# Eleven of the Vector engine's additions, between attention and the expert layer, given to GpSimd, with the order of stages kept

## The chip, the cores and the metric

The kernel runs on one core of one Trainium2 chip. The metric is the device time of one execution in microseconds (us), the median of three runs. In the rows and below, PE is TensorE, DVE is VectorE, ACT is ScalarE, POOL is GpSimd and SP is SyncE.

## The reference

The input x is 16 images of 64 channels and 16x16 pixels. A grouped, split-attention convolution block with a residual comes first. Its output is read as tokens: 256 pixels, each with 64 channels, for each of the 16 images. Over the images (axis 0 of `t`) runs a causal attention, then an expert layer with a router:

```python
x = _L0_conv_ref(x, ...)
t = _to_tokens(x)
t = t + _L1_attn_ref(_ln_t(t), L1_attn_fc_w, L1_attn_fc_b, L1_attn_score_w)
t = t + _L1_ffn_ref(_ln_t(t), L1_ffn_Wr, L1_ffn_br, ...)

def _causal_attend(H, e):
    # C[t] = sum over s<=t of softmax(e[s]) * H[s]
    ...
def _L1_ffn_ref(x, Wr, br, W1, ...):
    feat = jnp.mean(x, axis=0)
    w = jax.nn.softmax(feat @ Wr + br, axis=-1)
    h = jnp.einsum('bfd,edh->bfeh', x, W1) + b1
    ...
    return jnp.einsum('bfed,fe->bfd', y, w)
```

Two pieces matter here. The second layer norm works on the tokens with the attention's context added, centred over channels. The router works on the mean of the normalised tokens over the 16 images.

## The kernel before, in words

All arrays fit into the on-chip memory. The images are worked in four quarters, k = 0 to 3, of four images each. A quarter's token tensors are 128 partitions (pixels) by 512 elements (two halves of the pixels, q, by four images, by 64 channels).

One string, `ORDER` (L71 to L87), names every stage as `name.k`. Each engine walks through it and issues only those stages that it has a function for, so the string fixes the order of instructions on every engine. Engines meet only through semaphores. A wait holds everything behind it on the same engine.

The stages that matter for a quarter k:

- `ln1`, `hn`: first layer norm. ACT squares, DVE reduces (L675, L676), POOL raises the variance to the power -1/2 (`power`, L331), and DVE multiplies (L681) the centred tokens `xc` into `hn`.
- `hch`, `fc`, `score`: TensorE and ACT make the attention scores. `coef`, `att` (L690 to L708): DVE makes the coefficients and the first form of the context `ctxs`.
- `scan` (`scan_context`, L720): DVE adds the running context, image by image, in eight small instructions of 128x64. The last raises `ctx_ready`.
- `cen` (`add_to_centred`, L727): `xc` += `ctxs`, 128x512, and raises `centred2`.
- `ln2`: ACT squares the new `xc` (`squares2`, L423), DVE reduces it (L675), POOL takes the power (L331). `xn2`: DVE multiplies (L681) `xc` into the normalised tokens.
- `xt`: TensorE transposes them (L943), ACT copies them into `xs` (L428).
- `xr` (`sum_pairs`, L740 to L745): running sum of `xs` over image pairs, 128x256. Quarter 0 needs one addition and each other quarter two, `xpart` and then `xsum`. The last total feeds `logits` (TensorE L967), from which the routing weights are made.
- `l1.n`, `l2.n` (L1008, L1021): the first and second expert layers, 32 units each. Between them the ReLU is on ACT (L446), and for every second one of the first twenty on DVE (`d1.0` to `d1.9`, L753). ACT does the ReLU behind the second layer (L452).
- `mix` (DVE L783, TensorE L1033) weighs with the routing weights and applies the third layer, and `finish` (L790) adds up the result.

The part of the order around the change reads:

```python
    outp.3 hch.1 fc.1 heat.5 att.0 scan.0 gn4.3 heat.6 cen.0 hn.2 gn4f.3 ln2.0 x1.3 t2.0 hch.2 coef.1 xn2.0 score.1 att.1 tok.3 scan.1
    fc.2 d1.0 xt.0 cen.1 l1.0 l1.1 ln1.3 d1.1 xc.3 score.2 ln2.1 l1.2 l1.3 l2.0 l2.1 coef.2 l1.4 l1.5 hn.3 l2.2 l2.3 d1.2 att.2 xn2.1
    hch.3 l1.6 scan.2 l1.7 fc.3 xt.1 cen.2 d1.3 xr.0 ln2.2 l2.4 l2.5 score.3 l1.8 coef.3 d1.4 l1.9 l2.6 xr.1 l2.7 l1.10 l1.11 l2.8 xn2.2
    l2.9 d1.5 att.3 d1.6 l1.12 scan.3 cen.3 l1.13 l2.10 d1.7 l2.11 xt.2 ln2.3 l1.14 l1.15 l2.12 l2.13 l1.16 d1.8 xn2.3 l1.17 l2.14 l2.15
    l1.18 l1.19 d1.9 xr.2 xt.3 l2.16 xr.3 l2.17 l1.20 l1.21 t2.1 logits.0 l2.18 l2.19 l1.22 l1.23 t2.2 wt.0 l2.20 l2.21 wb.0 wb.1 l1.24
```

Of the kernel before, what the change touches and what calls it, by code (L numbers as in the profile page):

```python
# [22 lines left out]
ALU = mybir.AluOpType  # L23
# [5 lines left out]
P = 128  # L29
# [13 lines left out]
Q = 2  # L43
# [4 lines left out]
BQ = B // NQ  # L48
# [41 lines left out]
def conv_attention_experts(nc: bass.Bass, x: bass.AP, params: bass.AP, row_params: bass.AP, conv1_w: bass.AP, out: bass.AP):  # L90
# [6 lines left out]
    with ExitStack() as ctx:  # L97
        def sb(name, shape, dt=F32):
            return ctx.enter_context(nc.sbuf_tensor(name, shape, dt))

        def sem(name):
            return ctx.enter_context(nc.semaphore(name))
# [26 lines left out]
        xc = sb("xc", [P, NQ, Q, BQ, C])  # L129
        ctxs = sb("ctxs", [P, NQ, Q, BQ, C])  # L130
        xs = sb("xs", [P, NQ, Q, PQ, P])
# [34 lines left out]
        def tile(name, rows, *dims):  # L166
            n = 1
            for d in dims:
                n *= d
            if name not in small_names:  # L170
                small_names[name] = sb("s_" + name, [P, n])
            t = small_names[name][0:rows, 0:n]
            if len(dims) == 2:
                return t.rearrange("p (a b) -> p a b", a=dims[0])
            if len(dims) == 3:
                return t.rearrange("p (a b c) -> p a b c", a=dims[0], b=dims[1])
            return t
# [12 lines left out]
        def sem_list(*names):  # L190
            return [sem(n) for n in names]
# [20 lines left out]
        tok_in_psum, square_ready, hn_ready, ctx_ready = sem_list("tok_in_psum", "square_ready", "hn_ready", "ctx_ready")  # L212
        hch_in_psum, hch_ready, fc_done, qch_ready = sem_list("hch_in_psum", "hch_ready", "fc_done", "qch_ready")
        exps_in, exps_ready = sem_list("exps_in", "exps_ready")
        centred_kept, centred2, square2_ready, xn2_ready = sem_list("centred_kept", "centred2", "square2_ready", "xn2_ready")
        ctx_turned, ctx_added = sem_list("ctx_turned", "ctx_added")
        xt_ready = sem("xt_ready")
        pairs_added, xsum_ready = sem_list("pairs_added", "xsum_ready")
        xs_ready = sem("xs_ready")
# [48 lines left out]
        def rstd(name):  # L268
            n, rows, cols = var_tiles[name]
            return tile(n + "r", rows, cols)  # L270
# [5 lines left out]
        def by_pixel_half(t, k):  # L276

            return t[:, pairs_of(k), :].rearrange("p i (q n) -> p q i n", q=Q)

        def flat(bank_):  # L280

            return bank_[:].rearrange("p (q i n) -> p q i n", q=Q, i=PQ)
# [9 lines left out]
        def merged(t, k):  # L292

            return t[:, k].rearrange("p q b c -> p (q b) c")
# [7 lines left out]
        def context_at(k, q, t):  # L302

            return 2 * (k * BQ + t - 1) + q + 1
# [5 lines left out]
        @block.sync  # L310
        def _(sp):
            for n in range(PAIRS // 2):
                pairs = slice(2 * n, 2 * n + 2)
                sp.dma_start(xin[:, pairs, :], x_pairs[pairs].rearrange("b p n -> p b n")).then_inc(x_loaded[n], 16)
            sp.dma_start(w1[:], conv1_w).then_inc(conv1_w_loaded, 16)
            sp.dma_start(par[:, n_early:], params[:, n_early:]).then_inc(params_loaded, 16)
            for s in range(STRIPS):
                sp.dma_start(row_par[s * STRIP:(s + 1) * STRIP], row_params).then_inc(rows_loaded, 16)

            for k in range(NQ):  # L320
                sp.wait_ge(res_ready, k + 1)
                sp.dma_start(out_pairs[pairs_of(k)].rearrange("b p n -> p b n"), res[:, pairs_of(k), :]).then_inc(out_stored, 16)
            sp.wait_ge(out_stored, 16 * NQ)

        @block.gpsimd
        def _(pool):
            G = nc.gpsimd
            def power(name):
                n, rows, cols = var_tiles[name]
                pool.wait_ge(var_ready, VAR_AT[name])  # L330
                G.tensor_tensor(rstd(name), tile(n, rows, cols), minus_half[0:rows, 0:cols], ALU.pow).then_inc(rstd_ready, 1)  # L331

            G.memset(warm[:], 0.0).then_inc(warm_ready, 1)  # L333
            G.memset(minus_half[:], -0.5).then_inc(consts_ready, 1)
            G.memset(ones[:], 1.0).then_inc(ones_ready, 1)
            for k in range(NK):
                G.memset(pad[:, k * PK:(k + 1) * PK], 0.0).then_inc(pads_zeroed, 1)
            pool.wait_ge(consts_ready, 1)
            for name, k in ORDER:
                if name == "gn1f":  # L340
                    power(("gn1", k))
                elif name == "bn":
                    power(("bnv", k))
                elif name in ("gn2f", "gn3f", "gnaf", "gn4f"):
                    power((name[:-1], k))
                elif name in ("ln1", "ln2"):
                    power((name, k))

        @block.scalar
        def _(act):  # L350
# [124 lines left out]
        def _(dve):  # L475
# [8 lines left out]
            V = nc.vector  # L484
# [5 lines left out]
            def group_finish(name, n, rows=P):  # L490

                t, _, _ = var_tiles[name]
                ms, sq = tile(t + "ms", rows, 2, n), tile(t + "sq", rows, n)
                dve.wait_ge(small_ready, SMALL_AT[name])
                V.tensor_copy(ms, bank[SMALL][0:rows, 0:2 * n].rearrange("p (a n) -> p a n", a=2)).then_inc(small_free, 1)
                dve.wait_ge(small_free, SMALL_AT[name])
                step(V.scalar_tensor_tensor(sq, ms[:, 0, :], 1.0, ms[:, 0, :], ALU.mult, ALU.mult))
                V.scalar_tensor_tensor(tile(t, rows, n), ms[:, 1, :], EPS, sq, ALU.add, ALU.subtract).then_inc(var_ready, 1)
# [221 lines left out]
                        V.scalar_tensor_tensor(ctxs[:, k, q, t], before, a_[:, q, t:t + 1], ctxs[:, k, q, t],  # L720
                                               ALU.mult, ALU.add).then_inc(ctx_ready, 1)

            def add_to_centred(k):

                dve.wait_ge(centred_kept, k + 1)
                dve.wait_ge(ctx_ready, context_at(k, Q - 1, BQ - 1))
                V.tensor_tensor(merged(xc, k), merged(xc, k), merged(ctxs, k), ALU.add).then_inc(centred2, 1)  # L727

            def add_context(k):

                dve.wait_ge(ctx_turned, 1)
                t = by_pixel_half(x1, k)
                V.tensor_tensor(t, t, flat(bank[CONTEXT]), ALU.add).then_inc(ctx_added, 1)

            def sum_pairs(k):

                dve.wait_ge(xs_ready, k + 1)
                total, part = tile(f"xsum{k}", P, Q, P), tile(f"xpart{k}", P, Q, P)
                if k == 0:
                    V.tensor_tensor(total, xs[:, k, :, 0, :], xs[:, k, :, 1, :], ALU.add).then_inc(xsum_ready, 1)  # L740
                else:
                    dve.wait_ge(xsum_ready, k)
                    V.tensor_tensor(part, xs[:, k, :, 0, :], tile(f"xsum{k - 1}", P, Q, P), ALU.add).then_inc(pairs_added, 1)
                    dve.wait_ge(pairs_added, k)
                    V.tensor_tensor(total, part, xs[:, k, :, 1, :], ALU.add).then_inc(xsum_ready, 1)  # L745

            def relu1(m):
                if (m, 1) in ON_DVE:
# [7 lines left out]
            def routing_weights():  # L756

                dve.wait_ge(small_ready, SMALL_AT["logits", 0])
                lg, mx = tile("lg", P, Q, E), tile("lmax", P, Q)
                V.scalar_tensor_tensor(lg, bank[SMALL][:, 0:Q * E].rearrange("p (q e) -> p q e", q=Q), 1.0 / B,  # L760
                                       w("br").rearrange("p (q e) -> p q e", q=Q), ALU.mult, ALU.add).then_inc(small_free, 1)
                dve.wait_ge(small_free, SMALL_AT["logits", 0])
                step(V.tensor_reduce(mx, lg, AX_X, ALU.max))
                V.tensor_tensor(lg, lg, each(mx, P, Q, E), ALU.subtract).then_inc(logits_ready, 1)
                ex, sm = tile("wexp", P, Q, E), tile("wsum", P, Q)
                dve.wait_ge(wexp_ready, 1)
                step(V.tensor_reduce(sm, ex, AX_X, ALU.add))
                step(V.reciprocal(sm, sm))
                soft = tile("wsoft", P, P)
                for s in range(STRIPS):  # L770
                    V.tensor_tensor(soft[:, s * STRIP:s * STRIP + Q * E].rearrange("p (q e) -> p q e", q=Q), ex,
                                    each(sm, P, Q, E), ALU.mult).then_inc(wt_ready, 1)

            def weights_turned():
                dve.wait_ge(small_ready, SMALL_AT["wt", 0])
                V.tensor_copy(tile("wT", P, P), bank[SMALL][:, 0:P]).then_inc(small_free, 1)
# [8 lines left out]
            def finish(k):  # L785
# [15 lines left out]
                "coef": attention_coefficients, "att": attend, "scan": scan_context, "ln2": lambda n: layer_norm_stats("ln2", n),  # L801
                "xn2": lambda k: layer_norm_scale("ln2", k, xn2_ready),
                "logits": lambda k: routing_weights(), "mix": weigh, "finish": finish,
                "wt": lambda k: weights_turned(), "xr": sum_pairs, "t2": lambda k: add_context(k) if k == 0 else None, "cen": add_to_centred, "d1": relu1,
            }
            for name, k in ORDER:
                if name in stages:
# [355 lines left out]
```

## Time and profile before

| What | Value |
|---|---|
| Time, median of 3 runs | 140.77 us (140.62 to 140.92) |
| Span of the profiled execution | 139.0 us |
| PE busy | 120.3 us (87%) |
| DVE busy | 110.3 us (79%), 379 instructions |
| ACT busy | 79.8 us (57%) |
| POOL busy | 33.8 us (24%), 34 instructions |

The span runs from the first to the last instruction of the profiled execution; the profile gives no other time for it. The median of the runs is 1.8 us longer than the span, which is what lies around the instructions. In the rows, a time of start is counted from the start of the span, and instructions of one line that follow each other are merged into one row, with their number. TensorE's 32-bit matmuls appear as two passes each, so "x8" is four of the program.

### The profile page before, as it was taken

Reading aid. Unit: us, or ns where it says so; the run is one execution under the profiler, and the core shown is the slowest. Engines: PE = TensorE matmul, PEld = TensorE weight load, DVE = VectorE, ACT = ScalarE, POOL = GpSimd, SP = SyncE. Lnnn points to the kernel's source line nnn. Section 1 sums busy time; section 2 is a strip of 40 time slices with the busy share of each in tenths; the row PEclk is TensorE's granted clock in tenths of the full one; section 3 lists DMA queues with packets and bytes.
Section 4 is the critical chain, followed back from the end, with each engine's and each line's share of the span. In section 5 each row is a group of like instructions: output and inputs, shape, how many; then the busy total and the mean of one; then the engine's idle time right before and its main releaser. Section 6 shows DMA issues by size and latency. Waiting matters only on the chain.

```text
span 139.0 us, 2634 instructions
## 1 busy us (share of the span) xinstructions
PE 120.3 (87%) x891; PEld 52.6 (38%) x891; DVE 110.3 (79%) x379; ACT 79.8 (57%) x172; POOL 33.8 (24%) x34
## 2 busy tenths in 40 slices
PE   6989699999973499899777899999699999999990
PEld 2333234443322363455264433544144542221320
DVE  0497878495588999999999999999775169999941
ACT  4003030399569859458454688789798994366300
POOL 8022362002503464246325062040130000000000
PEclk9999999999998556999999999999999999999999
DMA  4997000000000000000000000000000000020042
GB/s 81 386 419 194 0 2 5 0 0 5 0 2 5 0 0 2 0 0 0 0 5 0 0 0 2 5 0 0 0 0 5 0 0 0 5 78 2 0 151 75
DMA packets 2813, 4.96 MB, mean 36 GB/s; under 512 B 240, under 2 KB 2416, under 8 KB 2672
## 3 DMA queue, kind: packets, MB, share of 16 engines
q1 hardware_dynamic: 2656, 4.60, 9.5%
q10 hardware_dynamic: 144, 0.20, 0.8%
q8 instruction: 7, 0.11, 0.3%
q14 instruction: 6, 0.05, 0.1%
HBM read 3.75 MB, written 1.05 MB: 35 GB/s over the span
## 4 chain that ended last, share of the span: by engine, by line
PE 58%; DVE 31%; issue 4%; ACT 4%; POOL 2%; DVEq 0%; ACTq 0%; POOLq 0%
PE bank L1021 12%; PE bank L1008 12%; PE bank L1033 10%; PE bank L882 7%; PE bank L830 5%; DVE s_wst L602 4%; DVE y L654 3%; DVE hn L681 2%; DVE x L668 2%; PE bank L822 2%; PE bank L943 2%; DVE s_ln1sq L675 1%; ACT y L387 1%; PE bank L935 1%; PE bank L843 1%
## 5 line engine op out<-in xcount | busy, mean ns | idle before, releaser
L1008 PE MATMUL bank<-xs,f1s 64*64 64x512 f32 x128 | 19.6, 608 | 2.0 <-ACT h L446 1.2
L1021 PE MATMUL bank<-h,f2s 64*64 64x512 f32 x128 | 20.1, 604 | 0.0
L882 PE MATMUL bank<-pad,w 32*64 32x512 f32 x288 | 18.1, 598 | 0.3 <-DVE pad L560 0.3
L446 ACT ACTIVATE h<-bank,s_bnb 128x512 f32<-128x512 f32 x22 | 14.4, 687 | 5.0 <-PE bank L1008 5.0
L830 PE MATMUL bank<-warm 128*128 128x512 bf16 x32 | 10.3, 473 | 1.3 <-POOL warm L333 1.3
L359 ACT ACTIVATE act<-bank,par 128x512 f32<-128x512 f32 x4 | 2.7, 687 | 13.2 <-PE bank L843 13.1
L366 ACT ACTIVATE y<-bank,par 128x512 f32<-128x512 f32 x8 | 5.0, 681 | 8.9 <-PE bank L882 8.9
L882 PEld LDWEIGHTS bank<-pad,w 32*64 32x64 f32 x288 | 6.1, 130 | 7.4 <-issue 6.7
L1008 PEld LDWEIGHTS bank<-xs,f1s 64*64 64x64 f32 x128 | 5.2, 131 | 9.7 <-ACT h L446 4.8
L753 DVE TENSOR_SCALAR h<-bank,s_bnb 128x512 f32<-128x512 f32 x10 | 7.5, 746 | 1.4 <-PE bank L1008 1.4
L1021 PEld LDWEIGHTS bank<-h,f2s 64*64 64x64 f32 x128 | 5.5, 132 | 7.9 <-issue 3.9
L783 DVE TENSOR_TENSOR more<-more,wb 128x512 f32<-128x512 f32 x8 | 4.9, 686 | 3.0 <-ACT wb L460 3.0
L602 DVE TENSOR_REDUCE s_wst<-y 128x8 f32<-128x512 f32 x8 | 5.4, 676 | 1.9 <-ACT y L366 1.9
L374 ACT ACTIVATE more<-y 128x256 f32<-128x256 f32 x16 | 6.5, 413 | 0.0
L720 DVE SCALAR_TENSOR_TENSOR ctxs<-ctxs,s_coefa 128x64 f32<-128x64 f32 x30 | 6.2, 278 | 0.1
L911 PE MATMUL bank<-par,x 128*128 128x128 f32 x32 | 5.4, 321 | 0.8 <-DVE x L668 0.8
L830 PEld LDWEIGHTS bank<-warm 128*128 128x128 bf16 x32 | 3.6, 123 | 6.0 <-issue 3.3
L911 PEld LDWEIGHTS bank<-par,x 128*128 128x128 f32 x32 | 4.8, 225 | 2.2 <-ACT x L394 1.3
L896 PE MATMUL bank<-y,par 128*64 128x512 f32 x16 | 4.9, 691 | 0.8 <-DVE y L654 0.8
L452 ACT ACTIVATE y<-bank,s_bnb 128x512 f32<-128x512 f32 x8 | 5.0, 682 | 0.8 <-PE bank L1021 0.8
L517 DVE BATCH_NORM_STATS2 s_gn1v0raw<-xin 128x6 f32<-128x256 f32 x4 | 1.4, 414 | 4.9 <-DMA xin<-x 4.9
L452 ACT ACTIVATE more<-bank,s_bnb 128x512 f32<-128x512 f32 x8 | 5.0, 681 | 0.3 <-PE bank L1021 0.2
(296 smaller groups left out, 261.7 us busy)
## 6 DMA issues: line engine op xcount, KB each, us to landing
par<-params SPq DMA_DIRECT2D x1, 1516.0 KB, 9.0
xin<-x SPq DMA_DIRECT2D x4, 256.0 KB, 4.5
out<-act SPq DMA_DIRECT2D x4, 256.0 KB, 2.1
row_par<-row_params SPq DMA_DIRECT2D x4, 160.0 KB, 8.8
w<-conv_w SPq DMA_DIRECT2D x1, 288.0 KB, 5.0
par<-params ACTq DMA_DIRECT2D x1, 193.5 KB, 4.0
```

The costliest lines, as they stand in the source:

```text
L374: A.activation(more[:, u, i * PIX:(i + 1) * PIX], y[:, 2 * u + i, :], ACT.Square, accum_out=tile(f"wsum{k}", P, 2, BQ)[:, 1, s + i:s + i + ...
L446: A.activation(h1[n % 4][:], bank[Z1[h]][:], ACT.Relu, bias=tile("bnb", P, 3 * EP)[:, col:col + 1]).then_inc(h1_ready, 1)
L452: A.activation(held[n], bank[Z2[n % 2]][:], ACT.Relu, bias=tile("bnb", P, 3 * EP)[:, col:col + 1]).then_inc(h2_ready, 1)
L602: ins = V.tensor_reduce(tile(f"wst{u // 2}", P, BQ * WIN)[:, s * WIN:(s + 2) * WIN], y[:, 2 * u:2 * u + 2, :].rearrange("p s (a y c x) -> ...
L720: V.scalar_tensor_tensor(ctxs[:, k, q, t], before, a_[:, q, t:t + 1], ctxs[:, k, q, t], ALU.mult, ALU.add).then_inc(ctx_ready, 1)
L753: V.tensor_scalar(h1[(2 * m + 1) % 4][:], bank[Z1[1]][:], tile("bnb", P, 3 * EP)[:, col:col + 1], 0.0, ALU.add, ALU.max).then_inc(h1_by_dv ...
L830: T.matmul(bank[TURN][:], warm[:, 0:P], warm[:], start=True, stop=True)
L882: ins = T.matmul(bank[CONV1[k][2 * j + h]][at:at + C, :], w1[rows, tap, :], pad[rows, b:b + 2, dy:dy + S, dx:dx + S], start=(tap == 0), st ...
L911: ins = T.matmul(block_of(k, q, i), x1_block(k, q, i), w("centre"), start=True, stop=True)
L1008: ins = T.matmul(bank[Z1[h]][to, :], f1s[own, e, to], xs[own, k], start=True, stop=True)
L1021: ins = T.matmul(bank[Z2[h]][at:at + C, :], f2s[rows, h, e, :], h1[n % 4][rows, :], start=True, stop=True)
L1033: T.matmul(bank[OUT[k]][h * C:(h + 1) * C, :], wo[:, e, :], held[m], start=False, stop=(e == EP - 1)).then_inc(mlp_done, 1)
```

## The change

The functions `add_to_centred` and `sum_pairs` move from the DVE block into the POOL block, and the POOL loop calls them where `ORDER` has `cen` and `xr`. Waits, semaphores, operands and the string `ORDER` are as they were.

```diff
@@ POOL block @@
+            def add_to_centred(k):
+
+                pool.wait_ge(centred_kept, k + 1)
+                pool.wait_ge(ctx_ready, context_at(k, Q - 1, BQ - 1))
+                G.tensor_tensor(merged(xc, k), merged(xc, k), merged(ctxs, k), ALU.add).then_inc(centred2, 1)
+
+            def sum_pairs(k):
+
+                pool.wait_ge(xs_ready, k + 1)
+                total, part = tile(f"xsum{k}", P, Q, P), tile(f"xpart{k}", P, Q, P)
+                if k == 0:
+                    G.tensor_tensor(total, xs[:, k, :, 0, :], xs[:, k, :, 1, :], ALU.add).then_inc(xsum_ready, 1)
+                else:
+                    pool.wait_ge(xsum_ready, k)
+                    G.tensor_tensor(part, xs[:, k, :, 0, :], tile(f"xsum{k - 1}", P, Q, P), ALU.add).then_inc(pairs_added, 1)
+                    pool.wait_ge(pairs_added, k)
+                    G.tensor_tensor(total, part, xs[:, k, :, 1, :], ALU.add).then_inc(xsum_ready, 1)
...
+                elif name == "cen":
+                    add_to_centred(k)
+                elif name == "xr":
+                    sum_pairs(k)
@@ DVE block @@
-            def add_to_centred(k):
-
-                dve.wait_ge(centred_kept, k + 1)
-                dve.wait_ge(ctx_ready, context_at(k, Q - 1, BQ - 1))
-                V.tensor_tensor(merged(xc, k), merged(xc, k), merged(ctxs, k), ALU.add).then_inc(centred2, 1)
...
-            def sum_pairs(k):
...
-                "wt": lambda k: weights_turned(), "xr": sum_pairs, "t2": lambda k: add_context(k) if k == 0 else None, "cen": add_to_centred, "d1": relu1,
+                "wt": lambda k: weights_turned(), "t2": lambda k: add_context(k) if k == 0 else None, "d1": relu1,
```

On POOL, the queue from quarter 0's layer norm to the end stands in this order before (`s_gn4v3r`, `s_ln1v3r` and `s_ln2v0r` to `s_ln2v3r` are results of the power):

```order
L331 TENSOR_TENSOR s_gn4v3r<-s_gn4v3,minus_half 128x2
L331 TENSOR_TENSOR s_ln2v0r<-s_ln2v0,minus_half 128x8
L331 TENSOR_TENSOR s_ln1v3r<-s_ln1v3,minus_half 128x8
L331 TENSOR_TENSOR s_ln2v1r<-s_ln2v1,minus_half 128x8
L331 TENSOR_TENSOR s_ln2v2r<-s_ln2v2,minus_half 128x8
L331 TENSOR_TENSOR s_ln2v3r<-s_ln2v3,minus_half 128x8
```

The six are all that POOL has left to do there. With the change the last part of the same queue, from quarter 2's addition on, reads:

```order
L337 TENSOR_TENSOR xc<-xc,ctxs 128x512
L344 TENSOR_TENSOR s_xsum0<-xs 128x256
L331 TENSOR_TENSOR s_ln2v2r<-s_ln2v2,minus_half 128x8
L347 TENSOR_TENSOR s_xpart1<-xs,s_xsum0 128x256
L349 TENSOR_TENSOR s_xsum1<-s_xpart1,xs 128x256
L337 TENSOR_TENSOR xc<-xc,ctxs 128x512
L331 TENSOR_TENSOR s_ln2v3r<-s_ln2v3,minus_half 128x8
L347 TENSOR_TENSOR s_xpart2<-xs,s_xsum1 128x256
L349 TENSOR_TENSOR s_xsum2<-s_xpart2,xs 128x256
L347 TENSOR_TENSOR s_xpart3<-xs,s_xsum2 128x256
L349 TENSOR_TENSOR s_xsum3<-s_xpart3,xs 128x256
```

The powers for quarters 2 and 3 now have additions ahead of them and behind them. On DVE the stretch of quarter 3, from its scan to the router, is before:

```order
L720 SCALAR_TENSOR_TENSOR ctxs<-ctxs,s_coefa3 128x64 x8
L727 TENSOR_TENSOR xc<-xc,ctxs 128x512
L753 TENSOR_SCALAR h1_3<-bank3,s_bnb 128x512
L675 TENSOR_REDUCE s_ln2sq3<-square 128x8
L676 TENSOR_SCALAR s_ln2v3<-s_ln2sq3 128x8
L753 TENSOR_SCALAR h1_1<-bank3,s_bnb 128x512
L681 TENSOR_TENSOR hn<-xc,s_ln2v3r 128x512
L753 TENSOR_SCALAR h1_3<-bank3,s_bnb 128x512
L743 TENSOR_TENSOR s_xpart2<-xs,s_xsum1 128x256
```

and with the change (the DVE functions up to `scan_context` have line numbers higher by 22 there, the later ones by 4):

```order
L742 SCALAR_TENSOR_TENSOR ctxs<-ctxs,s_coefa3 128x64 x8
L757 TENSOR_SCALAR h1_3<-bank3,s_bnb 128x512
L697 TENSOR_REDUCE s_ln2sq3<-square 128x8
L698 TENSOR_SCALAR s_ln2v3<-s_ln2sq3 128x8
L757 TENSOR_SCALAR h1_1<-bank3,s_bnb 128x512
L703 TENSOR_TENSOR hn<-xc,s_ln2v3r 128x512
L757 TENSOR_SCALAR h1_3<-bank3,s_bnb 128x512
L764 SCALAR_TENSOR_TENSOR s_lg<-bank4,par 128x16
```

Only the additions are gone; nothing else moved, there or on PE and ACT.

## Rows read from the trace of the kernel before

**Rows 1.** The page: the chain that ended last, by engine

```profile
PE 58%; DVE 31%; issue 4%; ACT 4%; POOL 2%; DVEq 0%; ACTq 0%; POOLq 0%
```

**Rows 2.** Busy time by stretch: length, PE, PEld, DVE, ACT, POOL, PE's clock, DMA

```profile
75.60:98.80 23.20, 22.19 (x154) 9.65 (x154) 22.37 (x76) 17.85 (x32) 4.87 (x3) 1.00 0.00 1
98.80:112.30 13.50, 12.43 (x109) 5.97 (x113) 6.70 (x21) 12.54 (x23) 1.64 (x1) 1.00 0.00 1
```

**Rows 3.** The chain in order of time: start, length, piece

```profile
70.27 0.55 issue
70.82 0.69 DVE hn L681
...
99.15 0.68 ACT h L446
```

**Rows 4.** Instructions by tile (`xc`, `xs`): ns least/median/most, first and last start

```profile
L727 DVE TENSOR_TENSOR xc<-xc,ctxs x4: 685/692/693, 70.2 to 97.9; 128x512 f32<-128x512 f32 x4
...
L743 DVE TENSOR_TENSOR s_xpart<-xs,s_xsum x3: 415/415/425, 91.7 to 104.7; 128x256 f32<-128x256 f32 x3
```

**Rows 5.** Timeline of DVE: start, length, what, [idle before <- releaser]

```profile
49.46 0.88 DVE L668 SCALAR_TENSOR_TENSOR x<-x,s_gn4v0r,xin 128x256 f32<-128x256 f32 x2
...
70.13 0.17 DVE L520 SCALAR_TENSOR_TENSOR s_gn4v3raw<-s_gn4v3raw 128x4 f32<-128x4 f32 x1
...
80.80 0.74 DVE L753 TENSOR_SCALAR h<-bank,s_bnb 128x512 f32<-128x512 f32 x1
...
88.12 0.69 DVE L727 TENSOR_TENSOR xc<-xc,ctxs 128x512 f32<-128x512 f32 x1
...
89.72 0.68 DVE L675 TENSOR_REDUCE s_ln2sq<-square 128x8 f32<-128x512 f32 x1
...
92.50 0.68 DVE L681 TENSOR_TENSOR hn<-xc,s_ln2v2r 128x512 f32<-128x512 f32 x1
...
97.89 0.69 DVE L727 TENSOR_TENSOR xc<-xc,ctxs 128x512 f32<-128x512 f32 x1
...
101.92 0.69 DVE L681 TENSOR_TENSOR hn<-xc,s_ln2v3r 128x512 f32<-128x512 f32 x1
```

**Rows 6.** Timeline of ACT

```profile
88.84 0.63 ACT L423 ACTIVATE square<-xc 128x512 f32<-128x512 f32 x1 [0.99 <-DVE xc L727]
...
98.61 0.63 ACT L423 ACTIVATE square<-xc 128x512 f32<-128x512 f32 x1 [0.98 <-DVE xc L727]
...
103.68 0.60 ACT L428 ACTIVATE xs<-bank 128x512 f32<-128x512 f32 x1
```

**Rows 7.** Timeline of PE

```profile
80.03 0.59 PE L1008 MATMUL bank<-xs,f1s 64*64 64x512 f32 x2
...
99.87 1.19 PE L1008 MATMUL bank<-xs,f1s 64*64 64x512 f32 x8 [1.19 <-ACT h L446]
...
102.91 0.66 PE L943 MATMUL bank<-par,hn 128*128 128x128 f32 x4
...
105.87 0.51 PE L967 MATMUL bank<-par,s_xsum 128*128 128x8 f32 x4
```

**Rows 8.** POOL's instructions by line and form: busy us, mean ns, idle before

```profile
L337 POOL MEMSET pad<- 128x1296 f32 x2 | 2.3, 1177 | 0.0
...
L331 POOL TENSOR_TENSOR s_ln1v1r<-s_ln1v,minus_half 128x8 f32<-128x8 f32 x1 | 1.6, 1636 | 2.2 <-DVE s_ln1v L676 2.2
...
L331 POOL TENSOR_TENSOR s_gn4v1r<-s_gn4v,minus_half 128x2 f32<-128x2 f32 x1 | 0.7, 696 | 2.8 <-DVE s_gn4v L533 2.8
...
L334 POOL MEMSET minus_half<- 128x32 f32 x1 | 0.1, 124 | 0.0
```

**Rows 9.** Timeline of POOL

```profile
31.68 1.01 POOL L331 TENSOR_TENSOR s_gn3v0r<-s_gn3v,minus_half 128x4 f32<-128x4 f32 x1 [9.40 <-DVE s_gn3v L498]
...
49.60 1.36 POOL L331 TENSOR_TENSOR s_gn3v3r<-s_gn3v,minus_half 128x4 f32<-128x4 f32 x1 [3.01 <-DVE s_gn3v L498]
...
100.25 1.64 POOL L331 TENSOR_TENSOR s_ln2v3r<-s_ln2v,minus_half 128x8 f32<-128x8 f32 x1 [7.93 <-DVE s_ln2v L676]
```

More of the change, by code:

```diff
@@ L733, in add_context @@
                 V.tensor_tensor(t, t, flat(bank[CONTEXT]), ALU.add).then_inc(ctx_added, 1)
-            def sum_pairs(k):
[L737 to L745, printed above, removed]
             def relu1(m):
```

## The prediction, made before the changed kernel had been run

> **What bounds the kernel now.** I read the page's chain first. PE has 58% of it and DVE 31% [rows 1], so neither engine alone sets the time, and it must be asked stretch by stretch. The busy time by stretch shows the place of the change: from 75.6 to 98.8 us PE is busy 22.2 and DVE 22.4 of 23.2 us, ACT 17.9, and POOL 4.9 [rows 2]. From 98.8 on DVE is nearly free (6.7 of 13.5 us). The chain in order of time then tells which DVE work counts. Up to the start of the expert layers, DVE's queue is the path: quarter 0's addition to `xc` is in it, as the 0.55 us of "issue" before `hn` at 70.82 [rows 3]. The timeline of DVE shows that instruction's place, behind the small L520 at 70.13 [rows 5]. After that PE's queue is the path, but for one place. At 98.8 PE stands for 1.19 us until ACT's ReLU ends [rows 7], and that ReLU at 99.15 is in the chain [rows 3]. ACT was late because it had itself waited 0.98 us, at the head of its queue, for quarter 3's addition on DVE [rows 6]. So the fourth `cen` ends on the path, and its end moves the total one to one. The third is nearly so: ACT waits 0.99 us for it, at 88.84 [rows 6].
>
> "No change" below means within 0.2% (0.28 us), about what a measurement of this kernel can tell. The sum is made against the profiled span, 139.0 us. The median of the runs is 1.77 us longer, and I add the difference to the median as it is.
>
> **What the additions cost.** On DVE the four `cen` take 0.69 us each, and of these 0.60 are queue time (70.21 to 70.82). The seven halves of `xr` take about 0.42 [rows 4]. No row shows an addition on POOL. Its fills do show what one pass through its port costs: 1.177 us for 1296 elements and 0.124 for 32 [rows 8], so 0.83 ns an element and 0.1 us fixed. An addition reads two operands. If its write goes beside the reads, that is two passes: 0.85 us for 512 elements and 0.43 for 256. The fixed part is 0.1 us as in a fill, or 0.38 us as in a power (0.696 us at 2 elements, 1.636 at 8, so 0.157 an element [rows 8]). That gives 0.95 to 1.23 us, and 0.53 to 0.81. I take **1.2 and 0.7 us**, from the upper part, since an addition is a TENSOR_TENSOR as the power is. The ends kept for the range are DVE's own 0.69 and 0.42 below, and three passes with 0.38 us fixed above: 1.66 and 1.02. A power's cost per element is no bound, since raising to a power is most of it.
>
> The Trainium skill, GPSIMD Engine Reference, section 3.1, measures this addition at 1.96 times DVE's time. As an estimate that makes 1.35 us of DVE's 0.69, and the sum below would be 142.1 us in place of 141.8.
>
> **Do the two engines hold each other up?** The trace has one sign of it. The power of four elements takes 1.01 us at 31.68 but 1.36 at 49.60 [rows 9], while DVE runs two SCALAR_TENSOR_TENSOR with two operands from on-chip memory, 49.46 to 50.34 [rows 5]. POOL lost 0.35 us there. The reverse, DVE held by POOL, is seen nowhere, but POOL reads only 8 elements a row so far, where it will now read 1024. I take it that a DVE instruction with two such operands and a POOL addition exclude each other, and the later one waits. The bounds for one meeting are nothing and the whole addition.
>
> The Trainium skill, SBUF — State Buffer, section "Who interferes with whom", says the same as a rule: the two share a read interface, and whoever comes second blocks fully. By that rule, the trace agrees for POOL's side (0.35 us); without it the sum would be 140.6, the first rival.
>
> **The change step by step** (negative is earlier than before):
> 1. *First `cen`.* POOL can start when the scan ends, at 69.42, so 69.47 to 70.67. DVE is rid of 0.60 us. But L520 at 70.13 [rows 5] has two such operands and now waits for 70.6. `hn.2` starts at 70.7 in place of 70.82: **-0.1** at the entry to the expert layers.
> 2. *Second `cen`.* DVE is rid of another 0.60 us, but the ReLU at 80.80 [rows 5] needs PE's matmuls that end at 80.62 [rows 7]. So the lead is 0.25 us at most. No two-operand work of DVE lies beside this addition.
> 3. *Third `cen`.* It can start 0.25 us sooner than at 88.12 and takes 0.5 longer: 87.82 to 89.02. ACT's square follows (0.63), and the sum over it on DVE starts at 89.75, against 89.72 before [rows 5]. The lead is gone: **0.0**. What DVE saved in between (0.60 for this `cen`, 0.33 for `xr.0`) is waiting time.
> 4. *`xr.1`.* It stood before `xn2.2` at 92.50 [rows 5]. Without it `xn2.2` could start when the power is there, at about 92.4. But on POOL the first half of `xr.1` stands directly behind that power, from 92.3 to 93.0, and reads while DVE wants to. `xn2.2` starts at 92.95: **+0.4** after rounding. DVE has no idle time from there to the fourth `cen`, so all of it arrives there.
> 5. *Fourth `cen`.* 1.2 in place of 0.69: **+0.5**. With step 4 it ends 0.9 later than before. ACT's square, the ReLU behind it and PE follow. Step 1's -0.1 is no help, since DVE's queue and not PE's leads here.
> 6. *`xn2.3`.* The power for it (100.25 [rows 9]) ends 0.9 later, at 102.8. Before, `xn2.3` at 101.92 [rows 5] was done at 102.61 and PE came for it at 102.91 [rows 7], 0.3 to spare. If the first half of `xr.2` goes first on POOL, `xn2.3` runs from 103.4 to 104.1 and PE waits 0.3; if DVE goes first, nothing. I count half: **+0.15**.
> 7. *`xr.3` and the router.* ACT's last copy ends 1.05 later, at 105.33 (103.68 + 0.60 before [rows 6]). Two halves on POOL end at 106.8; PE comes to the logits at 105.87 + 1.05 = 106.92 [rows 7]. **0.0**, with 0.1 us of cover. `xr.2` is done by 104.8. If that cover goes, every 0.1 us of POOL's half costs 0.2.
>
> Everything after the logits shifts with them. The sum is 0.4 + 0.5 + 0.15 = 1.05 us: 140.77 + 1.05 = **141.8 us**. The 2.7 us of DVE time that are freed (3 x 0.60 + 0.33 + 0.6 of waiting) buy nothing, as POOL's answer comes later at the two places where ACT stands waiting. PE's clock is at its upper level, 2.4 GHz (1.00), all through here [rows 2], and I count no change of it.
>
> **The rivals.**
> - *No holding up, and the additions at 1.2.* Step 1 gives -0.6, step 2 a lead of 0.85. The third `cen` costs 0.5 of it, less 0.2 us of slack behind the square (it ends at 89.47, DVE comes at 89.72): -0.54. Without `xr.1`, `xn2.2` is 0.66 early, and the fourth `cen` ends at -0.66 + 0.51 = -0.15. For it: DVE shows no lengthened instruction beside a power. Against: the 0.35 us. Time 140.6, no change.
> - *A cheap addition: faster.* The one mechanism is that POOL's pass is as fast as DVE's (0.69 and 0.42), so that nothing behind `cen` comes later. Then PE enters the expert layers 0.6 us sooner and the fourth `cen` ends 0.95 sooner, where PE's own matmuls stop the lead. Time 139.9. It decides at about 1.1 us without holding up, and at 0.85 with it. For it: a fill of 512 elements would take only 0.53. Against: two operands.
> - *A dear addition*, 1.66 and 1.02. Steps 3 and 5 cost 0.46 more each, step 4 0.32 more, step 6 its whole 0.3 and as the cover at the logits goes another 0.5: about +3.1. Time 143.9.
>
> **How the numbers follow.** The forecast has a chance of 0.50, the first rival 0.20, the cheap addition 0.13, the dear one 0.17. The forecast's own range is 141.1 to 142.6, by one meeting more or less and the addition between 1.05 and 1.35. The range for 8 in 10 is 140.2 to 143.1: it takes in the first rival, leaves out most of the cheap case and the worst part of the dear one. Faster: 0.13 and a third of the first rival, 0.19. Same: the rest of the first rival and a little of the forecast, 0.20. Slower: 0.61.
>
> **What would show it.** Right: `xc` additions on POOL of 1.1 to 1.3 us; ACT's waits before the squares of quarters 2 and 3 longer than 0.99 and 0.98; PE's wait of 1.19 for the ReLU now near 2; `hn` of quarter 2 starting at the end of an `xpart`; PE's logits matmuls with no wait for `xsum`. Wrong: additions under 0.9 us, or DVE's two-operand instructions at the same length and start beside them, would give the time away to a rival; a wait of PE for `xsum`, or a fall of PE's clock after 75 us, would be costs that I have at nothing.

## The result, and the profile after

The changed kernel takes 143.50 us (median of 4 executions, 142.72 to 143.63), against 140.79 for the kernel before (now four executions). The medians are 2.7 us apart; the ratio worked out from all executions, which isn't the quotient of the medians, is 1.0169 (95% interval 1.0135 to 1.0203) and makes 2.4 us. It is slower by either. The forecast said slower, by 1.05 us, in a range that ended at 143.1. The sign held and so did the mechanism on POOL, DVE and ACT; the size did not, and a cost of TensorE's clock came on top.

One of the four executions stands apart, and it is the profiled one: 142.72 us at a mean granted clock of TensorE of 0.964. The other three took 143.45 to 143.63 us at 0.951 or 0.952. So there are two questions: where the profiled execution lost 1.9 us (span 140.9 against 139.0), and what cost the other three another 0.8 us. (The kernel before had a mean clock of 0.963 in its profiled execution.)

The page's line of chain shares, to set beside [rows 1]:

```profile
DVE 41%; PE 37%; issue 7%; POOL 6%; ACT 4%; DMA 3%; POOLq 0%; DVEq 0%
```

DVE leads the chain now, although it does less, and POOL has 6% in place of 2%. Not all of PE's drop is the change: at the start of the kernel the chain goes over a load (DMA, 3%) here, where before it went over PE's warm-up matmuls (5%). Busy time by stretch, against [rows 2]:

```profile
75.60:98.80 23.20, 21.69 (x154) 9.24 (x154) 20.24 (x71) 17.76 (x31) 10.02 (x9) 1.00 0.00 1
98.80:112.30 13.50, 11.01 (x93) 5.01 (x91) 5.50 (x16) 10.94 (x19) 6.04 (x6) 1.00 0.01 1
```

DVE is rid of 2.1 us in the first stretch (22.37 to 20.24), and PE loses 0.5 us there and 1.4 us in the second all the same. The timeline of POOL in the profiled execution, where no addition stood before:

```profile
69.67 1.26 POOL L337 TENSOR_TENSOR xc<-xc,ctxs 128x512 f32<-128x512 f32 x1 [2.45 <-DVE ctxs L742]
...
88.13 1.27 POOL L337 TENSOR_TENSOR xc<-xc,ctxs 128x512 f32<-128x512 f32 x1 [4.10 <-DVE ctxs L742]
...
92.69 0.73 POOL L347 TENSOR_TENSOR s_xpart<-xs,s_xsum 128x256 f32<-128x256 f32 x1
93.50 1.05 POOL L349 TENSOR_TENSOR s_xsum<-s_xpart,xs 128x256 f32<-128x256 f32 x1
...
98.71 1.26 POOL L337 TENSOR_TENSOR xc<-xc,ctxs 128x512 f32<-128x512 f32 x1 [4.16 <-DVE ctxs L742]
...
106.83 0.73 POOL L349 TENSOR_TENSOR s_xsum<-s_xpart,xs 128x256 f32<-128x256 f32 x1
```

An addition of 512 elements costs 1.26 us and one of 256 costs 0.73; I had taken 1.2 and 0.7. The `xsum` at 93.50 took 1.05, and the reason stands in the timeline of DVE beside it, against [rows 5] (in the changed kernel L703 is `hn`, L697 the sum over ACT's squares, L542 the small L520 of before, L757 the ReLU on DVE):

```profile
70.23 0.72 DVE L542 SCALAR_TENSOR_TENSOR s_gn4v3raw<-s_gn4v3raw 128x4 f32<-128x4 f32 x1
...
80.77 0.75 DVE L757 TENSOR_SCALAR h<-bank,s_bnb 128x512 f32<-128x512 f32 x1 [0.35 <-PE bank L1012]
...
90.10 0.69 DVE L697 TENSOR_REDUCE s_ln2sq<-square 128x8 f32<-128x512 f32 x1 [1.45 <-ACT square L445]
...
92.75 1.21 DVE L703 TENSOR_TENSOR hn<-xc,s_ln2v2r 128x512 f32<-128x512 f32 x1 [0.57 <-POOL s_ln2v2r L331]
...
103.32 1.22 DVE L703 TENSOR_TENSOR hn<-xc,s_ln2v3r 128x512 f32<-128x512 f32 x1
```

`hn`, 0.68 us before, shows 1.21. POOL's `xpart` had begun 0.06 us ahead of it and ended at 93.42; `hn` ended at 93.96, a little under its own length later. Then `xsum`, issued at 93.50 while `hn` was still at work, ran until 94.55: 0.32 us more than the `xsum` at 106.83 that met nobody. Each waited for the other in turn. A blocked instruction keeps its early start in the record and grows in length. The same made 0.72 us of L520's 0.17 (L542 here) beside the first addition. The Trainium skill (SBUF — State Buffer, "Who interferes with whom") has it as a rule that the two contend there under an exclusive lock, and that the order of issue decides who blocks; the trace agrees, in both directions. ACT and PE, against [rows 6, 7]:

```profile
89.44 0.63 ACT L445 ACTIVATE square<-xc 128x512 f32<-128x512 f32 x1 [1.55 <-POOL xc L337]
...
100.01 0.63 ACT L445 ACTIVATE square<-xc 128x512 f32<-128x512 f32 x1 [1.59 <-POOL xc L337]
```

```profile
101.26 1.19 PE L1012 MATMUL bank<-xs,f1s 64*64 64x512 f32 x8 [2.18 <-ACT h L468]
...
104.68 0.63 PE L947 MATMUL bank<-par,hn 128*128 128x128 f32 x4 [0.31 <-DVE hn L703]
...
107.70 0.58 PE L971 MATMUL bank<-par,s_xsum 128*128 128x8 f32 x4
```

ACT's waits of 0.99 and 0.98 are 1.55 and 1.59. PE's wait of 1.19 is 2.18, and 0.31 before the transposes is new. The logits (L971) start 0.14 us after the last `xsum` on POOL has ended (106.83 + 0.73), and 0.58 us after the start of the group before them, where it was 0.49 (105.38 to 105.87); with them PE loses 0.17 us, up to the start of the next group. The profiles `again`, `xr_only` and `both_behind` have the same 0.14 to 0.15, so PE does wait for the sum here. After the logits nothing moves any more: PE starts its last group at 135.76 in place of 133.86, so +1.90.

### The profile page after: what moved, and what is told of

It is laid out like the page before. It is cut to its first block, busy times and chain, and to the rows that moved or that the text cites. A ratio compares the mean times of both kernels' runs of the same rounds, so it can differ in the third digit from the quotient of the medians.

```text
span 140.9 us, 2632 instructions
## 1 busy us (share of the span) xinstructions
PE 118.8 (84%) x889; PEld 52.1 (37%) x891; DVE 106.9 (76%) x368; ACT 79.9 (57%) x172; POOL 44.6 (32%) x45
## 3 DMA queue, kind: packets, MB, share of 16 engines
HBM read 3.75 MB, written 1.05 MB: 34 GB/s over the span
## 4 chain that ended last, share of the span: by engine, by line
DVE 41%; PE 37%; issue 7%; POOL 6%; ACT 4%; DMA 3%; POOLq 0%; DVEq 0%
PE bank L1037 10%; PE bank L886 7%; PE bank L1025 6%; PE bank L1012 6%; DVE hn L703 4%; DVE s_wst L624 4%; DVE y L676 3%; DVE ctxs L742 3%; DMA xin<-x 3%; DVE h L757 2%; DVE x L690 2%; POOL xc L337 2%; PE bank L826 2%; DVE ctxs L730 1%; DVE s_ln1sq L697 1%
## 5 line engine op out<-in xcount | busy, mean ns | idle before, releaser
L1012 PE MATMUL bank<-xs,f1s 64*64 64x512 f32 x128 | 19.1, 608 | 3.0 <-ACT h L468 2.2
L834 PE MATMUL bank<-warm 128*128 128x512 bf16 x32 | 9.6, 451 | 1.3 <-POOL warm L351 1.3
L337 POOL TENSOR_TENSOR xc<-xc,ctxs 128x512 f32<-128x512 f32 x4 | 5.1, 1268 | 14.9 <-DVE ctxs L742 14.9
L1012 PEld LDWEIGHTS bank<-xs,f1s 64*64 64x64 f32 x128 | 4.7, 131 | 11.1 <-ACT h L468 5.5
L757 DVE TENSOR_SCALAR h<-bank,s_bnb 128x512 f32<-128x512 f32 x10 | 7.5, 746 | 1.3 <-PE bank L1012 1.3
L900 PE MATMUL bank<-y,par 128*64 128x512 f32 x16 | 4.3, 618 | 1.5 <-DVE y L676 1.5
```

Of the source, the lines that this page charges most:

```text
L337: G.tensor_tensor(merged(xc, k), merged(xc, k), merged(ctxs, k), ALU.add).then_inc(centred2, 1)
L757: V.tensor_scalar(h1[(2 * m + 1) % 4][:], bank[Z1[1]][:], tile("bnb", P, 3 * EP)[:, col:col + 1], 0.0, ALU.add, ALU.max).then_inc(h1_by_dv ...
L834: T.matmul(bank[TURN][:], warm[:, 0:P], warm[:], start=True, stop=True)
L1012: ins = T.matmul(bank[Z1[h]][to, :], f1s[own, e, to], xs[own, k], start=True, stop=True)
```

## The experiments

Two theories stood to be told apart on several points. **A**: additions of 1.26 us stand in front of ACT's squares of quarters 2 and 3; POOL and DVE exclude each other; and the clock of TensorE falls after the longer wait. **B**: another cause on each point, as every expectation says.

### The changed kernel again

No edit. 

> The changed kernel once more, unaltered. Its four executions were 142.72 us (the profiled one, granted clock 0.964) and three times 143.45 to 143.63 (clock 0.951 to 0.952). Theory A (TensorE's clock): where TensorE stands over 2 us at about 99 us, the clock falls in most executions, and that costs the further 0.8 us; if this profile is of a slower execution it shows a stretch of clock 0.5 after 95 us that the kernel before lacks, and the stages up to 99 us at the same times. Theory B (the meetings of POOL and DVE fall out differently from run to run): a slower profile shows the clock at 1.00 after 66 us and other lengths of hn and of the additions.

Measured: 143.72 us (142.35 to 143.87, four executions), ratio 1.0195 (1.0148 to 1.0243). Again one execution is low (142.35) and three are high. This time the profiled one is of the high sort, clock 0.952, span 142.0. Its timeline of PE and its stretches (columns as in [rows 2]):

```profile
101.19 1.66 PE L1012 MATMUL bank<-xs,f1s 64*64 64x512 f32 x8 [2.19 <-ACT h L468]
102.41 2.14 PE L1025 MATMUL bank<-h,f2s 64*64 64x512 f32 x8
104.12 1.67 PE L1012 MATMUL bank<-xs,f1s 64*64 64x512 f32 x8
```

```profile
98.80:101.20 2.40, 0.21 (x6) 0.01 (x2) 0.95 (x2) 1.27 (x3) 1.10 (x1) 1.00 0.00 0
101.20:106.00 4.80, 4.80 (x27) 2.19 (x27) 1.99 (x5) 3.19 (x6) 3.40 (x3) 0.64 0.00 0
```

Up to the wait of 2.19 us the two profiles agree within 0.1 us. Behind it the granted clock is 0.64 on average from 101.2 to 106.0, that is 1.2 GHz for some 3.4 of the 4.8 us, where the first profile has 1.00. The same eight second-layer matmuls take 2.14 us in place of 1.32. The transposes of quarter 3 start at 105.72 in place of 104.68, and the span is 142.0 in place of 140.9. The clock is still at its upper level when PE starts again at 101.19; it is low from about 101.8 to 105.2. A fall of the clock just behind the wait is what this high execution has and the low one hasn't. The other five high ones were not profiled: they show the same mean clock (0.951 or 0.952), not the place.

### The additions of the context alone

```diff
# against the changed kernel
-                elif name == "xr":
-                    sum_pairs(k)
# and sum_pairs stands in the DVE block again
```

> Only the four additions of the context on POOL; the router's sums stay on DVE. Theory A (additions of 1.26 us, exclusion of two-operand DVE work, waits in front of ACT's squares): no lengthened hn for quarters 2 and 3, the wait of PE for the ReLU near 1.19 + 0.6 = 1.8 us, in all +0.7 us at an unchanged clock, 141.5 us. Theory B (the router's sums cost nothing, the additions of the context all of it): as the full change, +1.9 us at an unchanged clock.

Measured: 141.89 us (141.46 to 141.95) against 140.63 for the kernel before in the same set, so +1.3 us by the medians; ratio 1.0080 (1.0063 to 1.0097), and the clock at 0.963 in all four. (`ctxs` is 0.20 us late already at 68 us in this profile, before the change begins; less that, its span of 140.1 is 0.9 us longer than before.) PE's wait for the ReLU is 1.81 us, as A said, and `hn` is 0.69 in both quarters. One meeting stayed: the router's first sum on DVE took 1.11 us in place of 0.42 beside POOL's third addition, in a stretch where DVE had to wait for ACT anyway. The total is 0.4 us above A's 141.5, and well below the full change, so B falls.

### The router's sums alone

```diff
# against the changed kernel
-                elif name == "cen":
-                    add_to_centred(k)
# and add_to_centred stands in the DVE block again
```

> Only the router's sums on POOL; the additions of the context stay on DVE. Theory A (exclusion): hn of quarters 2 and 3 take 1.2 us in place of 0.69 beside the first half of a sum, in all +0.6 to +0.9 us, 141.4 to 141.7 us. Theory B (no exclusion; the long hn has another cause, such as the addition to xc just before): hn 0.69, and the freed DVE time brings -0.2 us, 140.6 us.

Measured: 142.01 us (141.78 to 142.68, the last one at a clock of 0.939), ratio 1.0112 (1.0085 to 1.0138), +1.4 us by the medians. Timeline of DVE:

```profile
83.82 0.87 DVE L716 TENSOR_TENSOR_SCAN s_runsum<-s_aexp,s_runsum 128x4 f32<-128x4 f32 x2
...
92.44 1.21 DVE L695 TENSOR_TENSOR hn<-xc,s_ln2v2r 128x512 f32<-128x512 f32 x1 [0.57 <-POOL s_ln2v2r L331]
```

The long `hn` is here with no addition to `xc` on POOL at all, so B falls. The loss is larger than A's 0.6 to 0.9, because a third meeting shows: POOL is free early enough to start `xr.0` at 83.94, where DVE's two small scans (0.35 us together before) take 0.87. Their elements number four; it is the wait that is long. The third addition, on DVE here, starts 0.5 us later for it, when the profiles are laid together at `ctxs`. So in this kernel the sums, which no engine needs before 105 us, cost no less than the four additions that ACT waits for: the medians are 0.1 us apart, and the spans, laid together in the same way, are 1.2 and 0.9 us longer than before.

### Work for TensorE in place of the wait

```diff
# against the changed kernel; "fill.0" stands behind "xt.2" in the order
+            def fill_wait(n):
+
+                pe.wait_ge(small_free, SMALL_AT["score", 3])
+                for _ in range(8):
+                    T.matmul(bank[SMALL][:], warm[:, 0:P], warm[:], start=True, stop=True)
```

> The full change with eight bf16 matmuls of TensorE's warm-up kind (0.216 us each, 1.7 us together) put into the place where it waits for ACT's ReLU at 99 us; they write a PSUM bank that nothing reads. Theory A (the slower executions come from the clock falling after that wait): all executions now near 142.7 us. Theory B (the spread has nothing to do with the wait): three of four still at 143.5 us.

Measured: 142.52 us (142.27 to 142.81), ratio 1.0133 (1.0116 to 1.0149), clock 0.960 to 0.964 in all four. Timeline of PE:

```profile
96.79 1.89 PE L840 MATMUL bank<-warm 128*128 128x512 bf16 x8
98.61 1.09 PE L1018 MATMUL bank<-xs,f1s 64*64 64x512 f32 x8
99.52 1.04 PE L1031 MATMUL bank<-h,f2s 64*64 64x512 f32 x8
101.01 1.19 PE L1018 MATMUL bank<-xs,f1s 64*64 64x512 f32 x8 [0.46 <-ACT h L468]
```

The useless matmuls stand ahead of units 14 and 15 and push them into the wait, of which 0.46 us is left. The work behind it starts at the same time (101.01, and the first addition on POOL at 69.42, in place of 101.26 and 69.67), and the low mean clock is gone: none of four executions, where the full change shows it in six of eight. Eight useless matmuls make the kernel 1.0 us faster at the median (143.50 to 142.52). So what the clock costs goes with the wait here, and the rest, +1.9 us, doesn't.

### Which of the additions cost

```diff
# against the kernel with the additions alone, in the POOL loop; the other two stand in the DVE block
-                elif name == "cen":
+                elif name == "cen" and k < 2:     # "cen01"; "cen23" has k > 1
                     add_to_centred(k)
```

> Only the additions for quarters 0 and 1 on POOL; those of quarters 2 and 3 and the router's sums on DVE, as before. Theory A (what costs is the longer addition in front of ACT's squares of quarters 2 and 3, and the meetings of quarter 2 and 3's hn with the sums): no loss, and since quarter 1's addition frees 0.6 us of DVE time and the first two quarters' squares have slack, -0.3 us, 140.4 us; PE's wait for the ReLU at 99 us stays near 1.2 us. Theory B (every addition on POOL costs its 0.57 us): +0.5 us or more.

> Only the additions for quarters 2 and 3 on POOL, the rest on DVE. Theory A: more than the whole loss of cen_only (+1.1 us measured), since the help of quarter 1's addition is missing: +1.0 to +1.4 us, 141.7 to 142.0 us, PE's wait near 1.8 us. Theory B: half the loss of cen_only, +0.5 us.

Measured: quarters 0 and 1 on POOL 140.56 us, ratio 0.9975 (0.9950 to 1.0001); quarters 2 and 3 on POOL 141.72 us, ratio 1.0054 (1.0026 to 1.0082). The kernel before, on the same chip, spread further than before: 18 of its 27 executions had a clock of 0.960 or more and a median of 140.78, nine had 0.939 to 0.951 and 141.56. Those alike in clock give -0.3 us for quarters 0 and 1 (140.45, nine executions), and +0.9 us for 2 and 3 (141.65, eight). PE's wait is 1.19 in the first and 1.81 in the second. So the last two additions carry the loss, as A said, though A's 1.0 is just missed. Two of the ten executions of quarters 2 and 3, and two of the eleven of quarters 0 and 1, had a clock of 0.952 or less. A repetition of the first kernel gave 140.76 against 140.80, ratio 0.9990 (0.9967 to 1.0014):

> The additions of quarters 0 and 1 on POOL once more, for a narrower interval. Theory A: -0.3 us against the kernel before. Theory B: no difference.

Its gain of 0.3 us isn't confirmed. What is clear is that these two cost nothing that can be measured, though they take the same 1.26 us each.

### The sums behind hn

```diff
# against the changed kernel, in sum_pairs
+                if k:
+                    pool.wait_ge(xn2_ready, min(k + 2, NQ))
                 pool.wait_ge(xs_ready, k + 1)
```

> The full change, but POOL waits before the sums of quarters 1, 2 and 3 until DVE has done hn of the next quarter (2, 3 and 3), so that no sum starts beside an hn. Theory A (exclusion): hn of quarters 2 and 3 take 0.69 us again, PE's wait of 0.3 us before the transposes of quarter 3 goes, its wait for the ReLU shrinks to about 1.8 us, and with it the clock's fall may go: 142.2 us at clock 0.963, -0.5 us in the profile against the full change. Theory B (the long hn comes from the addition to xc or from DVE itself): hn stays at 1.2 us, 143.5 us.

Measured: 142.78 us (142.37 to 144.29), ratio 1.0136 (1.0075 to 1.0196). Two of the four executions had a clock of 0.963 or 0.964 and took 142.37 and 142.39 us; the profiled one had 0.939 and 143.16 us, so only differences within it are read. Timeline of DVE:

```profile
93.41 0.69 DVE L705 TENSOR_TENSOR hn<-xc,s_ln2v2r 128x512 f32<-128x512 f32 x1 [0.57 <-POOL s_ln2v2r L331]
...
95.11 0.64 DVE L728 TENSOR_TENSOR s_coefa<-s_aexp,s_runsum 128x8 f32<-128x8 f32 x1
```

`hn` is at 0.69 again, and so is quarter 3's, and PE's wait before the transposes is gone. But the 0.5 us isn't won for the fourth addition. The second half of the sum now meets `s_coefa`, an instruction of 8 elements, which takes 0.64 in place of 0.17. From the third addition on POOL to the fourth it is 10.57 us here (88.79 to 99.36) and 10.58 in the full change (88.13 to 98.71). PE still waits 2.19 us for the ReLU. The meeting had only moved to a smaller instruction, at the same price. And of the 0.38 us that PE's stretch from the end of that wait to the transposes of quarter 3 is shorter (3.04 in place of 3.42), 0.17 is lost again on the way to the logits, since the held sums now end at 108.00 and PE waits for them; so the gain is 0.2 us where A had 0.5.

This profile also speaks on the clock, and against a simple rule. Here are PE's clock over the span in 40 slices, in tenths (the page of `before`, of `again` and of this run), then PE behind its wait of 2.19 us and the stretches around the other fall, in this run:

```profile
PEclk9999999999998556999999999999999999999999
...
PEclk9999999999996558999999999999869999999999
...
PEclk9999999999995556999999779999999999999999
```

```profile
101.91 1.19 PE L1014 MATMUL bank<-xs,f1s 64*64 64x512 f32 x8 [2.19 <-ACT h L470]
102.82 1.32 PE L1027 MATMUL bank<-h,f2s 64*64 64x512 f32 x8
...
69.00:79.70 10.70, 8.18 (x58) 5.45 (x60) 10.39 (x38) 5.69 (x11) 4.60 (x4) 1.00 0.01 2
79.70:83.10 3.40, 3.40 (x20) 1.38 (x15) 2.24 (x7) 1.37 (x4) 2.26 (x3) 0.50 0.00 0
```

All three have a low stretch around 42 to 56 us, before the change begins; here it is longer (mean clock from 42 to 56 us 0.51, against 0.63 before). There is a second fall at 79.7, where PE's longest wait since 71 us is 0.78 us. And behind the wait of 2.19 us there is none: the second-layer matmuls take 1.32 us there, as at the upper clock, where `again` has 2.14. So a low mean clock doesn't tell where the clock fell, a fall needs no wait of 2 us just before it, and such a wait isn't always followed by one.

### The place in ACT's queue

```diff
-... l2.11 xt.2 ln2.3 l1.14 l1.15 ...
+... l2.11 xt.2 l1.14 ln2.3 l1.15 ...
```

On the kernel before: 

> The kernel before, with one entry of the order moved: on ACT the ReLU of unit 14 stands ahead of the square of quarter 3 (l1.14 before ln2.3). Theory A (ACT's place in the queue behind the addition is what holds PE at 99 us): PE's wait of 1.2 us there goes, and part of it comes back as a wait for hn of quarter 3 before its transposes, in all -0.3 us, 140.4 us. Theory B (PE would wait for something else at the same time): no change, 140.7 us.

Measured: 140.67 us against 140.94, ratio 0.9972 (0.9948 to 0.9996). The 1.2 us wait is gone, and 0.38 us before the transposes of quarter 3 has come in its place. Those alike in clock say 140.60 against 140.78, so the gain is some 0.2 us, less than the expected 0.3. One of the eleven executions had a clock of 0.951, though the wait at 99 us is gone.

On the full change: 

> The full change with the ReLU of unit 14 ahead of the square of quarter 3 on ACT. Theory A (behind the ReLU's wait stands a second one, since quarter 3's hn needs addition, square, sum and power, and then meets a router's sum): PE no longer waits 2.2 us for the ReLU, but about 1.7 to 2.0 us before the transposes of quarter 3, so the span stays within 0.4 us of the full change. Theory B (the ReLU's place in the queue is all): the wait is gone and the full change is at 141.0 us or less.

Measured: 142.64 us (142.23 to 142.79), ratio 1.0112 (1.0076 to 1.0148), all four at a clock of 0.960 or more, span 141.0. Timeline of PE:

```profile
101.35 1.65 PE L1025 MATMUL bank<-h,f2s 64*64 64x512 f32 x8 [0.91 <-ACT y L474]
...
104.76 0.63 PE L947 MATMUL bank<-par,hn 128*128 128x128 f32 x4 [0.90 <-DVE hn L703]
```

The one wait of 2.18 us has become two of 0.9. The span is what it was (141.0 against 140.9), so B falls, and the wait before the transposes is 0.90 and not 1.7 to 2.0, since a second wait that A did not name took the rest. The low mean clock is gone with the long wait, in four of four.

Both edits that had looked like gains, together: 

> The two edits that gained together: the additions of quarters 0 and 1 on POOL, and on ACT the ReLU of unit 14 ahead of the square of quarter 3. Theory A (two separate waits were shortened): the gains add up, -0.5 us against the kernel before, 140.2 us where that has 140.7, at a clock of 0.96. Theory B (both gains were scatter between executions): no difference to before.

Measured: 140.56 us (12 executions, two of them at a clock of 0.951 or less) against 140.80, ratio 0.9980 (0.9953 to 1.0006). The sum of the gains is not there; no version was shown to beat the kernel before by more than the 0.3% of the single edit above.

## Why the prediction was right or wrong

Measured in the profiled execution, whose times are 0.09 us late already at 69 us, before the change begins (`ctxs` and the stage behind it), and by the prediction's own steps:

| Step | Predicted | Measured |
|---|---|---|
| 1, entry to the expert layers | -0.1 | 0.0 (`hn` at 70.87 less 0.09, before 70.82) |
| 2 and 3, sum after quarter 2's square | 0.0 | +0.3 (90.10 less 0.09, before 89.72) |
| 4, `xr.1` meets `hn` | +0.4 | +0.4 |
| 5, fourth addition | +0.5 | +0.6 |
| 6, `hn` of quarter 3 | +0.15 | +0.4 |
| 7, logits | 0.0 | +0.1 |
| the clock | 0 | 0 in this execution, +0.8 at the median of the four |

Step 1: the first addition freed 0.6 us and gave it back, by the meeting with L520 that was named.

Step 2 is where the sum first goes wrong. I gave DVE a lead of 0.25 us at the third addition, though the rows that I named leave 0.18 at most (80.80 less 80.62). PE's matmuls did hold the ReLU back, as said, and the lead left at 88 us was 0.1. The path from the scan's end to the addition was 0.13 us, where I had 0.05, and the addition 1.27 instead of 1.2. Step 3 is therefore mis-sized by 0.3, all of it small pieces on one chain.

Step 4 held in place and price: `hn` ends at 93.96, 0.69 later than before when the 0.09 is taken off, of which 0.3 is from step 3. Step 5: the fourth addition ended 1.3 us later than before (99.97 less 0.09 against 98.58), where I had 0.9. Step 6 I had counted at half because either engine could come first. POOL did, in both meetings of both profiles of the full change: its sum starts 0.06 or 0.07 us ahead of `hn` where both had waited for the power. The whole 0.3 was due, and a bit more. Step 7's cover of 0.1 us was used up: the last `xsum` ended 107.56, and PE's logits waited for it, which the prediction had named as a sign of being wrong. Steps 2 to 7 make the 1.8 us of the profiled execution; the forecast for it was 1.05.

The step that put the time outside the range was "I count no change of it", on the clock. I looked at the granted clock and saw 1.00 throughout, but I had worked out myself that PE's wait would grow to about 2 us, and had not asked what the clock does behind it. In six of eight executions the mean clock was 0.951 or 0.952 in place of 0.964, and in the one of them that was profiled it fell to 1.2 GHz for some 3.4 us, for 1.1 us of span. The two executions without it took 142.72 and 142.35 us, inside the range, though 0.6 to 0.9 us above the forecast, by the terms mis-sized in steps 3, 5, 6 and 7. The prediction did name a fall after 75 us as a cost that it had at nothing. That these two lie inside the range is in part luck: it reached to 143.1 for the sake of dear additions, which did not come.

The other mechanisms were right: ACT standing in front of the last additions, the exclusion in both directions, the unchanged stretch behind the logits. Of the rivals, "no holding up" is excluded by the long `hn`, by the sums alone and by `hn` at 0.69 where no sum runs beside it; the cheap and the dear addition by 1.26 us. (The dear one's terms add up to +2.9, not to +3.1, which changes no choice.) The factor of 1.96 of the Trainium skill (GPSIMD Engine Reference, section 3.1), given there for 2048 elements, is 1.83 here for 512 elements (1.26 to 0.69), and 1.74 for 256 (0.73 to 0.42).

That the wait of 2.2 us makes the low clock more frequent is what the counts say: six of eight executions of the full change with it and two of four with the sums behind `hn`, none of eight where it was filled or split. That it brings the fall by itself is not shown. In the sums behind `hn` it was followed by none, and another fall came at 79.7, 9 us after PE's last wait of over 0.8 us; and the kernel before, whose longest wait there is 1.19 us, had a low clock in 14 of 50 executions in two sets and in none of the seven of an earlier one. None of those 14 was profiled, so where their clock fell is open, and so is why two of the eight escaped.

## What to carry to other kernels

Work taken off a busy engine is worth only what its consumer gets earlier. Here the freed 2.1 us of DVE time ended as waiting, since two of four results came 0.6 us later to an engine that stood waiting for them at the head of its queue. Before giving elementwise work to POOL, list what DVE does beside it: an instruction with two operands from on-chip memory can take on the rest of the POOL instruction, and those of 4 and 8 elements here did. And where a change lengthens one wait of TensorE, put a price on the clock behind it too, and look at the clock of every execution and not only of the profiled one; splitting the wait, or filling it with useless matmuls, took that part away in four executions each.

## What was not expected of the hardware

- A DVE instruction of 4 or 8 elements went from 0.17 us to 0.64 and 0.72 beside a POOL addition. Both ended 0.02 us after POOL's, so the loss was what was left of POOL's instruction, whatever the size of what waited.
- A kernel with one wait of 2.2 us of TensorE had a low mean clock in six of eight executions, at a price of 0.8 us in the first four and 1.4 us in the second. In the profiled one, the clock fell from 2.4 to 1.2 GHz for some 3.4 us, 0.6 us after the wait had ended. With two waits of 0.9 us in its place no execution of four had it.
- The fall isn't tied to such a wait: one profile has the wait of 2.19 us with the clock at 1.00 behind it, and a fall at 79.7, where PE's last wait of over 0.8 us had ended at 70.9.
